# A graph network beside a mixer: each edge unit stored by two DMAs, of 112 and of 13 rows, in place of one of 125

## The reference

```python
xn = _layernorm(x, axis=-1)
x = x + gnn(xn, edges, ...) + mixer(xn, ...)      # 4 layers: linear attention, then an MLP of width 1024
x = x + lstm_head(_layernorm(x, axis=-1), ...)    # a recurrence over the 6250 rows
```

```python
scores = h_src @ a_s + h_tgt @ a_t
mx = segment_max(scores, tgt)
ex = exp(scores - mx[tgt])
se = segment_sum(ex, tgt)
agg = segment_sum(h_src * (ex / (se[tgt] + 1e-10))[:, None], tgt)
```

## Time and profile before

| what | value |
|---|---|
| time, median of 3 runs | 15123.15 us (15119.13 to 15126.68) |
| the profiled execution's own time | 15134.86 us |
| its span, first to last instruction | 15133.0 us |
| PE, VectorE, ScalarE, POOL busy | 85%, 45%, 46%, 20% of the span |
| mixer (layers 1 to 4) | about 0.30 to 4.07 ms |
| one layer: pass A, B, C | about 200, 253, 485 us |
| recurrence | from about 4.52 ms to the end |
| stores to `edge_tab` | 194, of 1391.1 KB (96), 758.8 KB (96) and 1138.2 KB (2) |
| gathers | 1650 indirect DMAs, 223.50 MB on their queue |
| mean granted TensorE clock | 0.957 |

### The profile page before, as it was taken

One profiled execution on the slowest core, in us unless ns is written; L12 is line 12 of the kernel. 1 busy time (PEld: TensorE's weight loads), 2 busy tenths in 40 slices (PEclk: granted clock), 3 DMA queues, 4 the chain that ended last, 5 costly groups with the idle time before them and its releaser, 6 DMA issues. The chain is left out here.

```text
span 15133.0 us, 1967100 instructions
## 1 busy us (share of the span) xinstructions
PE 12931.8 (85%) x904808; PEld 11428.5 (76%) x904808; DVE 6867.8 (45%) x47499; ACT 6946.3 (46%) x42309; POOL 2960.0 (20%) x4500
## 2 busy tenths in 40 slices
PE   3687776877669999999999999999999999999998
PEld 2566565766558888888888888888888888888886
DVE  4755747556553333333333333333333333333335
ACT  2454544645414444444444444444444444444443
POOL 4483764737700000000000000000000000000000
PEclk7898888988889999999999999999999999999998
DMA  3342543424420000000000000000000000000000
GB/s 80 97 143 71 148 123 98 145 72 144 136 94 3 2 2 2 2 2 2 2 2 2 2 2 2 2 2 2 2 2 2 2 2 2 2 2 2 2 2 19
DMA packets 673156, 542.56 MB, mean 36 GB/s; under 512 B 537744, under 2 KB 588954, under 8 KB 660765
## 3 DMA queue, kind: packets, MB, share of 16 engines
q1 hardware_dynamic: 450480, 316.45, 7.3%
q0 software_dynamic: 221600, 223.50, 6.1%
q10 hardware_dynamic: 934, 0.99, 0.0%
HBM read 286.52 MB, written 252.14 MB: 36 GB/s over the span
## 5 line engine op out<-in xcount | busy, mean ns | idle before, releaser
L1477 PE MATMUL p_g<-ring,wh 128*32 128x16 f32 x800000 | 8204.4, 186 | 700.3 <-DVE ring L1576 613.6
L1477 PEld LDWEIGHTS p_g<-ring,wh 128*32 128x32 f32 x800000 | 7592.2, 109 | 1475.3 <-DVE ring L1576 1156.3
L1518 ACT ACTIVATE cell<-p_g 128x3 f32<-128x3 f32 x12500 | 2181.8, 175 | 5555.5 <-PE p_g L1477 5555.5
L1570 DVE CUSTOM_DVE_ANT_1 cj<-cell 128x4 f32<-128x4 f32 x12500 | 2035.0, 163 | 5664.2 <-ACT cell L1518 5664.2
L1611 POOL COPY hist<-ring 128x6 f32 x2501 | 475.7, 190 | 10377.5 <-POOLq L1610 10377.5
L1521 ACT ACTIVATE tc<-cell 128x1 f32<-128x1 f32 x12500 | 2482.6, 199 | 0.0
L422 POOL DMA_INDIRECT eb<-node_tab,eidx x1650 | 2242.1, 1359 | 622.8 <-issue 448.3
L1576 DVE SCALAR_TENSOR_TENSOR ring<-og,tc 128x1 f32<-128x1 f32 x12500 | 1998.7, 160 | 774.8 <-ACT tc L1521 2.1
L1523 ACT ACTIVATE og<-p_g 128x1 f32<-128x1 f32 x12500 | 2043.2, 169 | 2.2 <-PE p_g L1477 2.0
L1451 PE MATMUL p_g<-xq,idn 128*32 128x24 f32 (+3 forms) x80032 | 1614.7, 189 | 61.4 <-PEq L1464 15.8
L1451 PEld LDWEIGHTS p_g<-xq,idn 128*32 128x32 f32 x80032 | 1254.4, 110 | 231.7 <-issue 15.9
(11 more groups left out here) (221 smaller groups left out, 6870.7 us busy)
## 6 DMA issues: line engine op xcount, KB each, us to landing
edge_tab<-eb SPq DMA_DIRECT2D x96, 1391.1 KB
edge_tab<-eb SPq DMA_DIRECT2D x96, 758.8 KB
eb<-node_tab,eidx POOLq DMA_INDIRECT x1650
xp_tab<-xo SPq DMA_DIRECT2D x50, 500.0 KB, 2.6
xq<-xp_tab SPq DMA_DIRECT2D x1251, 8.0 KB, 1.7
xq<-xp_tab SPq DMA_DIRECT2D x1250, 12.0 KB, 1.7
x<-w_in SPq DMA_DIRECT2D x8, 1024.0 KB
out<-ot SPq DMA_DIRECT2D x25, 250.0 KB
```

The costliest lines, as they stand in the source:

```text
L1477: m = pe.matmul(to[32 * q:32 * q + 32], wh[:, k, D * q + 32 * c:D * q + 32 * c + 32], ring[:, (s - 1) % TS, k:k + 1].broadcast_to([128, w] ...
L1518: act.activation(cell[:, s, k, 0:6:2], gate_at(h, u, k)[:, :, 0], ACT.Tanh).then_inc(l_s[k], 1)
L1570: dve.tensor_tensor_reduce(cj[:, k, :].rearrange("p (a b) -> p a b", a=2), cell[:, s, k, 0:4].rearrange("p (a b) -> p a b", a=2), cell[:, ...
```

## The change

A unit is stored by two DMAs on SP, rows 0 to 111 and rows 112 to 124, each adding 16 to the slot's semaphore; what waits for a free slot waits for 32. All 194 stores change, nothing else does.

```diff
--- before.py
+++ after.py
@@ edge_gather
-                    pool.wait_ge(e_free[s], 16)
-                    pool.sem_inc(e_free[s], -16)
+                    pool.wait_ge(e_free[s], 32)
+                    pool.sem_inc(e_free[s], -32)
@@ edge_store
-                    sp.dma_start(edge_pj[:, ds(c0, n), :], eb[s][:, 0:n, :]).then_inc(e_free[s], 16)
+                    for rows in by_rows:
+                        sp.dma_start(edge_pj[rows, ds(c0, n), :], eb[s][rows, 0:n, :]).then_inc(e_free[s], 16)
@@ the program of POOL
                     for s in range(NSLOT):
-                        pool.nop().then_inc(e_free[s], 16)
+                        pool.nop().then_inc(e_free[s], 32)
...
                     for s in range(NSLOT):
-                        pool.wait_ge(e_free[s], 16)
-                        pool.sem_inc(e_free[s], -16)
+                        pool.wait_ge(e_free[s], 32)
+                        pool.sem_inc(e_free[s], -32)
```

## The result

| | before | after |
|---|---|---|
| time, median (range; 7 runs each) | 15123.15 us (15118.55 to 15126.68) | 15072.11 us (15066.40 to 15075.68) |
| ratio, 95% interval | | 0.9966 (0.9954 to 0.9977) |
| the profiled execution | 15134.86 us | 15067.92 us |
| its span | 15133.0 us | 15066.1 us |
| mixer's end, where POOL goes on | 4072.97 us | 4009.11 us |

51 us or 0.34% faster. The forecast was 15085 us, -38 us. Lines from 508 on have moved by one.

A forecast was written before the change was run, and what follows sets the result against it. VectorE was taken to bound pass B, POOL's gather issue pass C. Terms -22 (lead), -9 (slot waits), +28 (hold), -32 (last lag), -3 (mixer's end) sum to -38 us: 15085 us from 15123.15, range 15040 to 15124 us.

The forecast's parts named there:

- rival 1: Pass C: the hold of POOL keeps its present mean of 2.3 us, so the +28 goes: -66 us, 15057 us; chance 0.13.
- POOL sets the pace in pass C: Pass C goes at POOL's pace of issuing gathers, 17.5 us a unit plus a hold by VectorE's run of 2.1 to 2.5 us.
- 125 rows on 5 engines, 112 on 16: Stores: 125 rows lie 25 deep on 5 DMA engines; split, 16 and then 13 engines hold them 8 deep.
- The store's duration: An 11-column store alone falls from 10.6 us to 4.5 us, between bounds of 3.4 and 7.2 us.
- SP and semaphores at nothing: 194 more DMA issues on SP, some 0.5 us each, and semaphore counts of 32 for 16 cost 0.
- Lead and slot waits: POOL starts each pass C 5.5 us sooner, -22 us; slot waits at pass C's start in layers 2 to 4 shrink, -9 us.
- The hold per unit: Pass C: VectorE's run stands fixed against POOL's gathers and holds every fourth one, 2.6 us lost, 20.15 us a unit: +28 us.
- Rival 2: Pass C: with lag above 3.6 us the hold falls to its short end, 1.6 us: -80 us more, about 15005 us; chance 0.05.
- a unit below 19.5 us: Sign in the new profile: a pass C unit this short, or a lag staying at 10 us, would make the forecast wrong.
- The lag of the last unit: End of each pass C: from last gather's issue to L431, 11.5, 10.0, 11.6 and 10.9 us fall to 3.05: -32 us.
- Rival 4: Long gathers come from full DMA queues and vanish with the stores: a further -208 us, 14877 us; chance 0.04.
- Rival 6: 134 GB/s limits the path, not five engines, so every gather waits for the store: +128 us, 15251 us; chance 0.06.

The follow-up runs named there:

- runs 4 to 8: Pass C on before/changed kernel: one gather less per unit, 15019.83/14964.26 us; three drains in VectorE's run, 14983.75/14892.0 us; changed kernel, two copies moved into that run, 14893.63 us.
- run 1: Changed kernel with stores split into 115 and 10 rows instead of 112 and 13: 15126.88 us, ratio 1.0003 to the kernel before.
- run 3: Changed kernel with only the 6-column stores of pass B split, those of pass C undivided: 15127.43 us, ratio 1.0001 to the kernel before.
- run 8: Changed kernel with two one-input copies moved from before the sums to after columns 5 and 8, pass C only: 14893.63 us, ratio 0.9849.
- run 6: Changed kernel with three VectorE drains in its run of L488 instructions, after columns 4, 6 and 8, pass C only: 14892.0 us, ratio 0.9849.

## Why the prediction was right, point by point

The time came within 13 us of the forecast, but it lies nearly as close to rival 1 (15057 us), and by the terms of the two traces the gain is 64 us, rival 1's 66. What speaks for the forecast's mechanism is the trace: the last lag is 3.0 us in every layer, and the units got longer, which rival 1 excludes. That the sum came so near was in part luck: terms were off by 3 to 17 us, not all to the same side, and the two profiled executions lie 16 us further apart than the medians.

- **POOL sets the pace in pass C.** Right; runs 4 to 8 show it from both sides.
- **125 rows on 5 engines, 112 on 16.** Right, by the packets and by run 1. The rule that splitting by partitions isn't worth it (the Trainium skill, DMA: Bandwidth & Descriptors, Rules for kernel authors) does not carry over to 125 partitions: the ratio is 0.9966. The page writes it of two halves that both spread over all 16 engines, which 125 rows on five do not. In run 1, where the part of 115 rows stays on five engines, a split gains nothing.
- **The store's duration.** 6.6 us, not 4.5. I kept the 26.8 GB/s of an engine among five for sixteen; together they reached 267 GB/s. The upper bound, 7.2 us from the `xp_tab` row, was the nearer one.
- **SP and semaphores at nothing.** Right: no term of the table needs them.
- **Lead and slot waits** (-31 forecast, -23 measured). The lead is 3.5 us a layer, not 5.5, since POOL gets its slot 4.7 us after the store's issue (3.7 us from first packet to last) and not after the 2.6 that I used. And the two are one chain (run 3), which the sum hid.
- **The hold per unit** (+28 forecast, +11.5 measured). The mechanism came out as written: lag 3.0 us in all layers, the fourth gather held until 0.76 us after L501, and the long units at 20.16 us in the mean against the 20.15 worked out. The step that failed is "the fourth starts inside [the run]" as a rule for every unit: 10 of 80 slip past and the fifth gather is held instead, for 1.1 us; 10 such units, 1.5 us shorter each, are 15 of the 16.5 us. Rival 2 had this case, but for all units or none. The prediction's own sign against it, a unit below 19.5 us, stands in these ten units and not in the others.
- **The lag of the last unit, -32.** Exact.
- **The mixer's end.** -6 for -3.
- **Missing: from layer to layer, -15.** The prediction followed engines that wait for semaphores only. The row at 2191.05 with 10.22 us of idle time stood in the trace of before, and the prediction has no term for it.
- **Rival 4** (long gathers vanish with the stores) fell: there were 95 gathers over 1.8 us before and 100 after. **Rival 6** fell too: 134 GB/s was a limit of five engines. But it was nearer than its chance says, as the sixteen stop at about twice that rate, not at three times.

Up to the mixer's end the profiled executions differ by 26 us more than the sum: 15 from layer to layer, 16.5 of give-back that did not come and 3 at the end, less 8 at pass C's start. The medians differ by 13 us more than forecast. The range and the direction held.

## What to carry to other kernels

Look at how many DMA engines a transfer occupies before its bytes: 125 partitions go to 5 engines, and a split into 112 and 13 doubles the rate. Then ask who waits for its end: here only the slot, the last unit and the branch to the next layer, so 194 shorter stores gave 0.34%, while two copies moved into a run of two-input VectorE instructions gave another 1.2% (run 8), because POOL's issue was the pace.

## What the runs showed that I had not expected

- VectorE's L488 takes two inputs from SBUF, and gathers that were held end 0.76 us after the L501 that follows a run of 14 such instructions, up to 3.2 us later than their 1.21 us would have it. The Trainium skill, SBUF — State Buffer (Who interferes with whom), states that a VectorE instruction with two SBUF inputs contends with a GpSimd instruction that reads SBUF; the traces agree, though no run changed the number of inputs by itself. They add that the hold lasts to the end of the back-to-back run, and that a drain (run 6) or a one-input copy of 0.17 us (run 8, 1.29 and 1.34 us per gather) inside the run ends it.
- Five engines moved 134 GB/s, sixteen with gathers and a store in flight 260 to 267 GB/s.
- Without any semaphore, a branch back took VectorE 6.0 to 7.4 us with an undivided 11-column store in flight (before) and 3.0 to 3.6 us without a store (after).
- A gather that begins inside VectorE's run is held or not by where it begins within one L488: of the fourth gathers, 61 at 0.00 to 0.12 us were held and ten at 0.13 to 0.18 us passed.
